# A post-norm transformer layer on one core: the first loads, the low-rank factors and the first turns put in another order

## The reference

```python
def lora_linear(x, W, b, Bm, Am):              # x (2, 1024, 512), W (512, 512)
    out = einsum('bld,od->blo', x, W) + b
    upd = einsum('blr,or->blo', einsum('bld,rd->blr', x, Bm), Am)   # Bm (16, 512), Am (512, 16)
    return out + 0.5 * upd

q = split(lora_linear(x, Wq, bq, Bq, Aq)); k = split(lora_linear(x, Wk, ...)); v = split(lora_linear(x, Wv, ...))
attn = softmax(q @ k.T * HEAD_DIM ** -0.5) @ v
x = layernorm(x + lora_linear(attn, Wo, bo, Bo, Ao))
x = layernorm(x + moe(x, ...))                 # 8 experts, capacity 256, plus a shared expert
```

## Time and profile before

| | us |
|---|---|
| median of three runs | 1038.34 (1038.18 to 1038.36) |
| the profiled execution | 1039.01 |
| span in its trace | 1037.4 |
| TensorE busy | 1011.8, 98% of the span |
| VectorE / ScalarE / GpSimd busy | 724.8 / 554.6 / 545.4 |

### The profile page before, as it was taken

How to read it: one execution, slowest core, us unless ns; L and a number is a source line. 1 busy time by engine, 2 the same in 40 slices (tenths; PEclk the granted TensorE clock), 3 DMA queues, 4 the chain that set the end, 5 groups by cost and what they waited for, 6 DMA issues and landing times.

```text
span 1037.4 us, 16141 instructions
## 1 busy us (share of the span) xinstructions
PE 1011.8 (98%) x5570; PEld 728.0 (70%) x5570; DVE 724.8 (70%) x1205; ACT 554.6 (53%) x970; POOL 545.4 (53%) x309
## 2 busy tenths in 40 slices
PE   6999999999999999999999999999999999999996
PEld 5877565555665656565446668788899999998885
DVE  4549878988888988888887578624666666763164
ACT  3321566666666666666665653523456566663116
POOL 2200689989898998989999842272000000004500
PEclk9999999999999999999999999999999999999999
DMA  8954432536237161423532566363577777775604
GB/s 268 329 145 137 125 93 67 128 71 153 72 82 183 37 150 39 113 72 82 131 134 74 163 181 186 122 166 62 134 214 222 230 221 230 220 217 108 95 1 162
DMA packets 162181, 145.74 MB, mean 140 GB/s; under 512 B 42481, under 2 KB 125681, under 8 KB 161856
## 3 DMA queue, kind: packets, MB, share of 16 engines
q1 hardware_dynamic: 154576, 128.36, 44.6%
q0 software_dynamic: 6656, 15.93, 5.6%
q10 hardware_dynamic: 880, 0.56, 0.2%
HBM read 84.70 MB, written 35.67 MB: 116 GB/s over the span
## 4 chain that ended last, share of the span: by engine, by line
PE 85%; DVE 5%; DMA 4%; ACT 2%; issue 2%; SPq 1%; ACTq 0%; DVEq 0%
PE bank L832 18%; PE bank L990 13%; PE bank L938 11%; PE bank L1003 11%; PE bank L1140 9%; PE bank L926 8%; PE bank L1048 4%; PE bank L898 3%; PE bank L1015 3%; DMA raw<-in_L_ffn_W_dram 2%; PE bank L839 2%; DVE w2lo L1795 1%; DMA at0lo<-attn_d 1%; PE bank L1117 1%; DVE mx L1654 1%
## 5 line engine op out<-in xcount | busy, mean ns | idle before, releaser
L1378 ACT ACTIVATE prob<-bank 128x512 f32<-128x512 f32 x512 | 289.5, 597 | 148.4 <-PE bank L990 117.0
L761 POOL TENSOR_TENSOR psum<-psum,prob 128x1024 f32<-128x1024 f32 x156 | 367.3, 2392 | 0.0
L1654 DVE TENSOR_REDUCE mx<-bank 128x1 f32<-128x512 f32 x512 | 322.8, 679 | 54.6 <-PE bank L938 53.7
L990 PE MATMUL bank<-Qs,Ks 97*128 97x512 f32 x512 | 201.3, 418 | 1.0 <-DMA Qs<-mrow 0.9
L938 PE MATMUL bank<-Ks,Qs 96*128 96x512 f32 x512 | 182.6, 405 | 1.9 <-DMA Qs<-plane_qhi 1.1
L990 PEld LDWEIGHTS bank<-Qs,Ks 97*128 97x128 f32 x512 | 95.8, 188 | 84.7 <-issue 36.4
L811 POOL DMA_DIRECT2D oe_d<-oe_sb x16 | 8.7, 546 | 227.9 <-ACT oe_sb L1515 226.8
L1003 PE MATMUL bank<-prob,V 128*32 128x512 f32 x1024 | 122.9, 597 | 0.0
L938 PEld LDWEIGHTS bank<-Ks,Qs 96*128 96x128 f32 x512 | 96.9, 189 | 33.1 <-issue 6.7
L926 PE MATMUL bank<-xThi,Wsl 128*128 128x512 f32 x256 | 99.9, 398 | 0.8 <-DVE plane_klo L1644 0.8
L761 POOL TENSOR_TENSOR psum<-prob,prob 128x1024 f32<-128x1024 f32 x32 | 75.8, 2388 | 45.2 <-PE bank L1015 39.1
(11 more groups left out here) (257 smaller groups left out, 2078.6 us busy)
## 6 DMA issues: line engine op xcount, KB each, us to landing
raw<-in_L_ffn_W_dram SPq DMA_DIRECT2D x120, 256.0 KB, 3.7
Ks<-plane_khi SPq DMA_DIRECT2D x64, 128.0 KB, 2.8
Qs<-plane_qhi SPq DMA_DIRECT2D x64, 128.0 KB, 2.3
raw<-in_L_ffn_sw_dram SPq DMA_DIRECT2D x30, 256.0 KB, 3.8
xin<-in_L_attn_x_dram SPq DMA_DIRECT2D x16, 256.0 KB, 5.3
v_d<-v_sb POOLq DMA_DIRECT2D x16, 256.0 KB, 3.6
Ks<-plane_klo SPq DMA_DIRECT2D x32, 128.0 KB, 2.5
Qs<-plane_qlo SPq DMA_DIRECT2D x32, 128.0 KB, 2.3
```

The source lines that it names most:

```text
L761: po.tensor_tensor(psum[:, pr], (prob[0] if kc == 1 else psum)[:, pr], prob[kc % RING][:, pr], ALU.add).then_inc(sem("sum_done"), 1)
L990: nc.tensor.matmul(score_at(v, i), Ks[v.b][0:97, hh, kc * P:(kc + 1) * P], Qs[v.b][0:97, hh, v.hf * HALF:(v.hf + 1) * HALF], start=True, s ...
L1378: ACTV(prob[kc % RING][:, hh, :], score_at(v, i), ACT.Exp, scale=SCALE).then_inc(sem("exp_done"), 1)
L1654: ins = RED(mx[(hf + ahead) % 2][:, 4 * hh + qt, part:part + 1], src, AX.X, ALU.max)
```

## The change

**Loads.** A of v becomes the first load of SP's queue. The A of k, q and o follow there behind Wv's two halves, ahead of x tile 1. ScalarE's queue issues the B of v alone. Behind Wk, SP's queue now issues the B of k, the bias row of v, x tiles 2 and 3, then the B of q and of o and the bias columns, then x tiles 4 and 5.

**The work.** TensorE begins with 14 transposes of the identity into a spare bank as soon as the identity is there, and does 10 more behind x tile 0; their results are read by nobody. The string begins with A and B of v, one tile of x, two chunks of v; VectorE then (letter w, its alone) widens the A of k, q and o in `lora_a`; then the two other chunks, the three A, the second x tile and the first v projection. The B of k now stands behind x tile 2. The banks of the A change, and with them the waits that keep a bank from being overwritten. A chunk of k waits for all four A.

**GpSimd** waits for the four widened A before it sets the row of `Ks`. In the router, far behind, two copies use another semaphore with the same two waits.

```diff
-FIRST_ORDER = "AAAAB xx WWWW B V x WW V x WW B V x WW V x WW V x B V x V V".replace(" ", "")
+FIRST_ORDER = "AB x WW w WW AAA x V x B WW V x WW B V x WW V x WW V x B V x V V".replace(" ", "")
...
-        return bank[(7, 6, 3, 2)[n]]
+        return bank[(7, 7, 0, 4)[n]]
...
+        load_a(W_ORDER[0], "lora_first")
         load_x(0, 1)
         load_w(0)
+        for m in W_ORDER[1:]:
+            load_a(m, "lora_ld")
         load_x(1, 2)
         load_w(1)
-        for m in W_ORDER[1:]:
+        load_b(W_ORDER[1])
+        sp.dma_start(bv_bc[:], ...).then_inc(sem("second_ld"), 16)
+        load_x(2, 4)
+        for m in W_ORDER[2:]:
             load_b(m)
...
+        po.wait_ge(sem("a_wide"), 4)
         po.memset(f32(Ks[0][96:97, :, :]), 1.0).then_inc(sem("ks_ones"), 1)
...
+        def warm(count):
+            for _ in range(count):
+                nc.tensor.transpose(bank[5][:, 0:P], ident[:], ident[:])
...
+        warm(14)
...
-            pe.wait_ge(sem("a_lo"), n + 1)
+            pe.wait_ge(sem("a_lo"), 4 if n == 1 else n + 1)
...
-        for m in W_ORDER:
-            ac.dma_start(lora_c[:, m], ...).then_inc(sem("lora_ld"), 16)
```

More of the change, by code:

```diff
@@ L420, in load_b @@
             for r in range(0, RSTACK, RANK):
-                sp.dma_start(lora_b[r:r + RANK, m], Bm[m]).then_inc(sem("b_ld"), 16)
+                sp.dma_start(lora_b[r:r + RANK, m], Bm[m]).then_inc(sem("second_ld" if m == W_ORDER[1] else "b_ld"), 16)
         def load_w(n):
@@ L444, in store_w, with load_a @@
                     sp.dma_start(wt_d[W_ORDER[n], s][:, dc, :], f32(w_stage[i][s][:])).then_inc(sem(f"w_st{i}"), 16)
+        def load_a(m, name):
+            sp.dma_start(lora_c[:, m], Am[m].rearrange("(p c) r -> p c r", c=DC)).then_inc(sem(name), 16)
+        load_a(W_ORDER[0], "lora_first")
         load_x(0, 1)
         load_w(0)
+        for m in W_ORDER[1:]:
+            load_a(m, "lora_ld")
         load_x(1, 2)
         load_w(1)
-        for m in W_ORDER[1:]:
+        load_b(W_ORDER[1])
+        sp.dma_start(bv_bc[:], bias[2].rearrange("(o d) -> o d", o=1).to_broadcast([P, D])).then_inc(sem("second_ld"), 16)
+        load_x(2, 4)
+        for m in W_ORDER[2:]:
             load_b(m)
@@ L454, in _ @@
                          bias[m][0:P].rearrange("(p o) -> p o", o=1)).then_inc(sem("qk"[m] + "_ld"), 16)
-        load_x(2, 4)
-        sp.dma_start(bv_bc[:], bias[2].rearrange("(o d) -> o d", o=1).to_broadcast([P, D])).then_inc(sem("bv_ld"), 16)
         load_x(4, 6)
@@ L846, in _, with turn_a @@
         pe.wait_ge(sem("const"), 2)
-        for n in range(4):
+        def warm(count):
+            for _ in range(count):
+                nc.tensor.transpose(bank[5][:, 0:P], ident[:], ident[:])
+        def turn_a(n):
             pe.wait_ge(sem("a_wide"), n + 1)
+            if n == 2:
+                pe.wait_ge(sem("x_lo"), 1)
+            if n == 3:
+                pe.wait_ge(sem("w_lo"), 1)
             for c in range(DC):
@@ L867, in weights @@
                     pe.wait_ge(sem("w_lo"), k - 1)
-                elif k >= 2:
-                    pe.wait_ge(sem("a_lo"), 4)
                 for oc in range(DC):
@@ L881, in turn_x @@
                     pe.wait_ge(sem("w_lo"), DC)
+                if t == 4:
+                    pe.wait_ge(sem("a_lo"), 3)
                 if t >= 4:
@@ L889, in make_v @@
                 pe.wait_ge(sem("x_lo"), t + 1)
-                if t == 0:
+                if t == 1:
                     pe.wait_ge(sem("a_lo"), 2)
@@ L901, in make_v @@
                 mm.then_inc(sem("v_mm"), 1)
-        x, k, t = 0, 0, 0
+        x, k, t, na = 0, 0, 0, 0
         for w in FIRST_ORDER:
-            if w == "x":
+            if w == "A":
+                turn_a(na)
+                na += 1
+            elif w == "x":
                 turn_x(x, x + 1)
                 x += 1
+                if x == 1:
+                    warm(10)
             elif w == "W":
@@ L1298, in b_factor @@
             m = W_ORDER[n]
-            ac.wait_ge(sem("b_ld" if n else "b_ld_first"), 16 * (RSTACK // RANK) * (3 if n else 1))
+            ac.wait_ge(sem(("b_ld_first", "second_ld", "b_ld", "b_ld")[n]), 16 * (5, 6, 10, 10)[n])
             ACTV(bs[0:RSTACK, m], lora_b[0:RSTACK, m], ACT.Identity).then_inc(sem("b_hi"), 1)
@@ L1315, in turned_x @@
                 turned(t // 4, t % 4, bank[t % 4], ("x_t", 0), "x_hi")
-        for m in W_ORDER:
-            ac.dma_start(lora_c[:, m], Am[m].rearrange("(p c) r -> p c r", c=DC)).then_inc(sem("lora_ld"), 16)
         for r in range(0, RSTACK, RANK):
@@ L1576, in _, with widen @@
         ve.wait_ge(sem("as_zero"), 1)
-        ve.wait_ge(sem("lora_ld"), 16 * 4)
-        for m in W_ORDER:
+        def widen(m):
             nc.vector.tensor_copy(lora_a[:, m, :, :, 0:RANK],
                                   lora_c[:, m].unsqueeze(2).to_broadcast([P, DC, 3, RANK])).then_inc(sem("a_wide"), 1)
+        ve.wait_ge(sem("lora_first"), 16)
+        widen(W_ORDER[0])
         def a_factor(n):
@@ L1632, in _ @@
                 k += 1
+            elif w == "w":
+                ve.wait_ge(sem("lora_ld"), 16 * 3)
+                for m in W_ORDER[1:]:
+                    widen(m)
             elif w == "V":
                 if t == 0:
-                    ve.wait_ge(sem("bv_ld"), 16)
+                    ve.wait_ge(sem("second_ld"), 16 * 6)
                 make_v(t)
@@ L1854, in _ @@
         parts = bank[6][:, 0:2 * NT * E].rearrange("p (t s e) -> p t s e", s=2, e=E)
-        nc.vector.tensor_copy(r3["lg"][:], parts[:, :, 1]).then_inc(sem("lg_read"), 1)
-        ve.wait_ge(sem("lg_read"), 1)
-        TT(r3["lg"][:], parts[:, :, 0], r3["lg"][:], ALU.add).then_inc(sem("lg_read"), 1)
-        ve.wait_ge(sem("lg_read"), 2)
+        link(nc.vector.tensor_copy(r3["lg"][:], parts[:, :, 1]))
+        link(TT(r3["lg"][:], parts[:, :, 0], r3["lg"][:], ALU.add))
         link(RED(r2["mx"][:], r3["lg"][:], AX.X, ALU.max))
```

## The result

The changed kernel is slower: 1041.38 us (median of 22 runs, 1038.19 to 1044.96) against 1038.58 for the kernel before on the same chip (22 runs, 1037.70 to 1042.32), a ratio of 1.0023 with a 95% interval of 1.0016 to 1.0029. The forecast was 1035.2. The profiled execution took 1041.18, its span 1039.6 against 1037.4: 2.2 us longer.

The account below looks back on a forecast made before the run. The prediction took TensorE's 9.5 us wait at the start as the bound: T = 8.0 plus 10.15 puts k's first chunk at 18.2 instead of 21.42, so 3.1 us off 1038.34 gives 1035.2, range 1034.3 to 1037.3.

Parts of the forecast that it names:

- What bounds the kernel: Whole run: TensorE's one outstanding wait is 9.5 us at the start; starting earlier by d ends the kernel earlier by d.
- The TensorE branch: Start: identity turns from 1.8, A and x turns, clock up at 7.1 to 7.6, TensorE free at about 7.9.
- T: Time at which v's first chunk starts on TensorE: forecast 8.0, ends 7.5 and 10.1, against 15.23 before.
- The B branch: Start: fifth B of v lands at 6.5 (6.0 to 8.6), then 1.5 us on ScalarE and VectorE, so T is 8.0.
- rival 1: Start: the B of v is not faster alone, T is 9 to 10.1, time 1036.1 to 1037.2; chance 0.17.
- From T to the first v projection: Prologue: four chunks, a 0.35 us wait, turns of three A and x tile 1; projection starts at T + 4.8.
- rival 3: Start: idle turns do not raise the clock and the 2.15 us pause lets it fall; 1038.2 or 1041.1; chance 0.06.
- Rival 3's slow case: Prologue: the clock also falls at the 2.15 us pause, 2.9 us more, time 1041.1; half of rival 3's 0.06.
- The projection, x tile 2 and the pause: Behind v's first projection: 2.80 + 0.44 us, then TensorE stands 2.15 us; k's first chunk at T + 10.15 = 18.2.
- The sum: k's first chunk moves from 21.42 to 18.2, 3.2 us; 3.1 taken, giving 1035.2.
- rival 2: First 50 us: a load, x tile 2 above all, or a store becomes the wait; price 1.0 to 3 us; chance 0.13.
- The parts at no cost: Fill of `Ks` from T + 3.5 to T + 7, k's wait for all A, router copies, earlier Wq issue: no cost.

Follow-up runs that it names:

- The kernel that was 3.0 us ahead at 49 us: Changed kernel with two of v's five B loads issued by SyncE, k's B ahead of v's first projection and no idle turns, second run: ratio 0.9964, 1036.13 us.
- the second trace of before: The kernel before run once more, unchanged, as a yardstick for how two traces of one program differ: ratio 0.9998.
- the split: Changed kernel with two of the five B of v loads issued by SyncE behind A of v, three by ScalarE: ratio 0.9997, 1040.11 us.
- the trace without the fall: The changed kernel run once more, unchanged, its clock not falling in the start: ratio 1.0029 against the kernel before.

## Why the prediction was wrong

The forecast was 3.1 us faster, and the kernel is 2.8 us slower. Two steps of the sum failed in the prologue, the landing of the B of v and the clock behind it, and a third term, what the change does to the rest of the run, was taken as nothing.

**What bounds the kernel** held in part: a start can carry through. The kernel that was 3.0 us ahead at 49 us, with no idle turns in TensorE's program, ended 3.6 us ahead. "A start that is earlier by d should end the kernel earlier by d", however, has an exception that the prediction did not think of: the work behind is the same, but not where its instruction loads and SyncE's pauses fall.

**The TensorE branch** was right: free at 7.65 (7.9), the 14 turns in 3.25 (3.0), the ten in 1.09 (between 1.1 and 2.1), the clock up at 6.30 (7.1 to 7.6), with nothing before it but turns. The forecast of the rise came from one trace; from TensorE's first turn to the rise it was 5.9 us there, 3.9 in the second trace of before, and 4.0 to 5.6 in the kernels with idle turns. This did no harm to the sum, because the B of v and not TensorE set T. The rule that transposes do not raise it (the Trainium skill, TensorE: Matmul & The Clock Gate, Part 4: PE-mode transpose) did not hold here either.

**The B branch** is the first step that failed. I took a landing at 6.5, near the lower end, reading the A of before as "a queue that is served in turns": "what made the B late was the backlog of its own queue, which is gone". The last B landed at about 8.4, near the upper end of 8.6, and T was 9.92 (ends 7.5 and 10.1). With that backlog gone the last B still took 5.4 us, because the DMA engines were filled by x and Wv from SyncE, as the split and its third B show. Cost: 1.9 us. This was rival 1, at a chance of 0.17. The rule of the Trainium skill beside it (DMA: Bandwidth & Descriptors, Issuing engines are not separate DMA queues), by which T would be 10.1, agrees with this trace.

**From T to the first v projection** was forecast at 4.8 and took 6.33. In the trace without the fall it took 5.06, so 1.3 us of the 1.5 are the lower clock level and the rest is there at the full one. This was the second failing step, the second half of rival 3. I held against it that at the end of the kernel the clock fell 4.5 us after TensorE stopped; in after it fell 2.1 us after TensorE stopped, and in three more kernels within 0.7 us behind a rest of 2.2 to 2.5. One fall at one place was too little to set a point from which it decides. The B's delay made the rest in which it fell, so rivals 1 and 3 were not separate cases. Rival 3's slow case names 1041.1, nearly the measured 1041.38; that is a coincidence, since it wanted turns that do not raise the clock and 2.9 us of low clock behind the pause, and neither was there.

**The projection, x tile 2 and the pause** were right: 2.79 + 0.44, and 2.17 us (2.15) ahead of k's first chunk. The 21.6 that was measured is the forecast with the two failed steps in it: 18.2 + 1.9 + 1.5.

**The sum** then is 0.2 us lost instead of 3.2 gained at k's first chunk. The rest of the difference, 1.7 to 3.8 us in the two traces, lies behind it, as in rival 2, but not by its mechanism: no load or store of the first 50 us became late. It is 0.5 us at 77 us (SyncE's pause), 0.6 to 1.2 at 378 us, and 0.7 to 1.0 behind 786 us (the load in a slice's flight). The last was shown by moving the loads, the first by moving the pause; the middle one is tied to the loads by their places and times, and no run was made to part the ways in which they could do it. About 0.4 (first trace) and 1.5 (second) fell between 850 and 918 us and have no explanation. Between 546 and 600 us 0.2 to 0.7 is regained in most traces, that of before, again, too, so there it is the first trace of before that was slow.

**The parts at no cost** were: the fill of `Ks` (at T + 4.8, not T + 3.5) and the router's copies are in no wait of TensorE. The moved issues were not free: the prediction counted them in landing times alone, but with four more rows on SyncE its pause comes four DMAs earlier in the work.

## What to carry to other kernels

A small transfer that gates the start should be issued ahead of the large ones on whatever queue, since a queue of its own does not shield it from traffic of the others; issued so, the B of v took 2 us instead of 5.4. When a wait in the prologue is removed, look for where the next 2 us of rest on TensorE will be, because work that is put in to raise the clock is lost if such a rest follows. And a gain of one to three microseconds from added or removed instructions has to be read in the trace to its end: every row that is added to TensorE's or SyncE's program moves later instruction loads and pauses, and those cost 0.2 to 3 us at places that have nothing to do with the change.

## What the runs showed of the hardware

- The granted clock fell in or within 0.7 us behind rests of TensorE of 2.2 to 2.5 us in the prologue (after; the kernel with 30 turns; the split one; the one with A on ScalarE's queue), and 0.9 us behind one of 1.9 us at 580 us; it did not fall at rests of 2.2 and 2.6 us of other executions. A fall in the prologue cost 1.3 to 1.6 us.
- Turns raised the clock with no other work before them, those of the identity alone in the kernel before with 42 of them (at 7.28 us, against 12.80 and 15.38 without). In after it rose at 6.30 and 5.71, without its idle turns at 13.99 and 14.77.
- TensorE's instructions come in loads of 16 KB that share the DMA engines with the data. Kernels in which one fell into the flight of an awaited transfer lost 0.6 to 3.1 us there, the larger figure with a fall of the clock in it.
- SyncE pauses 0.45 us behind the 79th row of its program in every kernel, whatever DMAs are ahead of it.
- A wait that is met already is a row of TensorE's program too: 84 of them moved its instruction loads by 32 matmuls, 42 turns by 52.
